# All expert weights split within a layer's first sums, by halves, and shorter layer ends

## What is computed

```python
h = x @ W_in + b_in                                  # 3125 x 256
for l in range(3):
    agg = segment_sum(h[src], dst) / deg
    logits = concatenate([h, agg], -1) @ router_W[l] + router_b[l]
    vals, idx = top_k(logits, 2); gates = softmax(vals)      # over 8 experts
    weak = relu(einsum('nh,ehf->nef', agg, weak_W[l]) + weak_b[l])          # 4 experts, 256 -> 256
    sh = relu(einsum('nh,ehf->nef', agg, strong_W1[l]) + strong_b1[l])      # 4 experts, 256 -> 512
    strong = einsum('nef,efh->neh', sh, strong_W2[l]) + strong_b2[l]        # 512 -> 256
    moe = einsum('ne,neh->nh', gate_dense, concatenate([weak, strong], 1))
    h = h + sigmoid(h @ conf_W[l] + conf_b[l]) * moe
out = h @ W_out + b_out
```

## Time and profile before

| | us |
|---|---|
| median of 3 runs | 3216.36 (3214.8 to 3218.52) |
| the profiled execution | 3218.61, its span 3216.3 |
| granted TensorE clock, mean | 0.975 of full |
| PE busy | 2951.0 (92%) |
| DVE busy | 2189.7 (68%) |
| ACT busy | 914.5 (28%) |

### The profile page before, as it was taken

How to read it: one execution, slowest core, us unless ns; L and a number is a source line. 1 busy time by engine, 2 the same in 40 slices (tenths; PEclk the granted TensorE clock), 3 DMA queues, 4 the chain that set the end, 5 groups by cost and what they waited for, 6 DMA issues and landing times. The chain is left out here.

```text
span 3216.3 us, 47575 instructions
## 1 busy us (share of the span) xinstructions
PE 2951.0 (92%) x18761; PEld 1780.5 (55%) x18761; DVE 2189.7 (68%) x4024; ACT 914.5 (28%) x1695; POOL 18.1 (1%) x23
## 2 busy tenths in 40 slices
PE   2888889999988999999979999988999998999997
PEld 2566555555443545454545666654666664666665
DVE  7999555557227777776657767675767675676676
ACT  3788421114101000000032222233222233232222
POOL 2000000000000000000000000000000000000000
PEclk8899999999998999999989999999999999999999
DMA  5455366775006554544330000020000001000001
GB/s 127 139 151 150 110 192 210 223 230 165 22 9 184 157 171 150 182 145 127 88 106 3 4 3 4 3 82 4 4 7 4 3 27 60 3 4 3 4 3 42
DMA packets 310959, 265.85 MB, mean 83 GB/s; under 512 B 32767, under 2 KB 289409, under 8 KB 308174
## 3 DMA queue, kind: packets, MB, share of 16 engines
q1 hardware_dynamic: 296558, 259.28, 26.3%
q10 hardware_dynamic: 13760, 2.61, 0.4%
q0 software_dynamic: 416, 0.85, 0.1%
HBM read 172.67 MB, written 90.05 MB: 82 GB/s over the span
## 5 line engine op out<-in xcount | busy, mean ns | idle before, releaser
L1874 PE MATMUL psum<-r_wd,r_h 128*128 128x512 fp8e4 (+1 forms) x2600 | 568.4, 375 | 13.4 <-ACT r_h L229 12.9
L2483 PE MATMUL psum<-m_weights,x_nodes 128*128 128x256 f16 (+1 forms) x3600 | 419.7, 275 | 18.0 <-DVE m_wtmp L2267 16.4
L2464 PE MATMUL psum<-m_agg,m_weights 128*128 128x512 f16 (+2 forms) x2016 | 410.3, 356 | 21.7 <-ACT m_agg L2364 21.7
L2422 PE MATMUL psum<-counts,m_h 128*128 128x512 fp8e4 (+2 forms) x2100 | 417.6, 354 | 12.6 <-DVE m_h L2153 12.6
L1874 PEld LDWEIGHTS psum<-r_wd,r_h 128*128 128x128 f16 x2600 | 241.4, 97 | 307.5 <-issue 16.0
L2483 PEld LDWEIGHTS psum<-m_weights,x_nodes 128*128 128x128 f16 (+1 forms) x3600 | 353.7, 99 | 73.3 <-DVE m_wtmp L2267 16.5
L2422 PEld LDWEIGHTS psum<-counts,m_h 128*128 128x128 f16 x2100 | 206.2, 99 | 206.0 <-issue 18.8
L2364 ACT ACTIVATE m_agg<-psum,x_nodes 128x512 f32<-128x512 f32 (+2 forms) x336 | 238.2, 719 | 279.2 <-PE psum L2464 271.2
L2464 PEld LDWEIGHTS psum<-m_agg,m_weights 128*128 128x128 f16 x2016 | 194.9, 99 | 218.8 <-issue 32.7
L2376 ACT ACTIVATE m_hT<-m_hT,m_g 128x256 f32<-128x256 f32 x300 | 135.8, 502 | 552.4 <-DVE m_hT L2281 552.4
L2267 DVE SCALAR_TENSOR_TENSOR m_wtmp<-psum,x_nodes,m_bias 128x256 f32<-128x256 f32 (+1 forms) x300 | 144.9, 483 | 139.0 <-PE psum L2483 137.9
(11 more groups left out here) (312 smaller groups left out, 3328.3 us busy)
## 6 DMA issues: line engine op xcount, KB each, us to landing
r_wd<-packed_sym SPq DMA_DIRECT2D x120, 640.0 KB, 4.1
packed_counts<-strip SPq DMA_DIRECT2D x21, 1800.0 KB, 7.8
sym_blocks<-packed_counts SPq DMA_DIRECT2D x88, 384.0 KB, 4.4
packed_sym<-sym_blocks SPq DMA_DIRECT2D x84, 384.0 KB, 3.3
w_stage<-in_L_gnn_strong_W SPq DMA_DIRECT2D x12, 1024.0 KB, 6.6
m_weights<-in_L_gnn_strong_W SPq DMA_DIRECT2D x21, 512.0 KB, 4.7
x_parked<-x_nodes SPq DMA_DIRECT2D x2, 1600.0 KB, 5.9
x_nodes<-x_parked SPq DMA_DIRECT2D x2, 1600.0 KB, 6.5
```

Of the source, the lines that this page charges most:

```text
L1874: m = pe.matmul(bank[pair[b]][:, 0:2 * cw], h16[:, part, p0 + i, :], f_[:, 2 * b:2 * b + 2, :], start=(p0 + i == 0 and part == 0), stop=(p ...
L2422: m = pe.matmul(bank[kb][:, 0:cw], h16[:, part, i, kb * P:(kb + 1) * P], A[:, i, c_:c_ + cw], start=(i == 0 and part == 0), stop=(i == NT ...
L2464: m = pe.matmul(bank[4 + hh % 2][:, 0:cw], w_[:, i, kb, f * P:(f + 1) * P], agg16[:, j, kb, 0:cw], start=(x_ == 0), stop=(x_ == len(todo) ...
L2483: m = pe.matmul(bank[b_][0:r_, 0:H], s_[:, pa[0] * BANK + k * P:pa[0] * BANK + k * P + r_], w_[:, pa[1], f, :], start=(f == 0 and pa == PA ...
```

## The change

It does five things, all in `block_experts`:

1. All ten pieces of the weights are split within the first sums, on DVE behind the split of h and ahead of the scales and biases, on ACT ahead of the mean. Nothing is split in chunk 0.
2. Each piece is split by halves of 512 columns, two instructions on each engine. ACT's piece k waits only for the low part of the first half of piece k-1.
3. The scale takes one matmul (the maxima, spread to 128 columns, as weights; the identity moving) and one reduction over 128 columns on all partitions. ACT waits for the scale alone, not for the numbers made after it.
4. `turn(0)` moves ahead of the scale on PE and on ACT, and h is split in groups of 2, 3, 5, 5, 5, 5 tiles.
5. In the last chunk DVE's routing is cut in three: hidden blocks 0 and 1, first choice, block 2, second choice, block 3, gates. ACT does its four hidden blocks and then the exponential. And the maximum of the last chunk is taken tile by tile, each behind its last strong tile.

```diff
-                FIRST = 4
+                HALVES = (slice(0, SL // 2), slice(SL // 2, SL))
...
-                H5 = [slice(i, i + 5) for i in range(0, NT, 5)]
+                HG = [slice(i, j) for i, j in zip((0, 2, 5, 10, 15, 20), (2, 5, 10, 15, 20, NT))]
...
-                    vec.wait_ge(max_turned, l + 1)
-                    vec.tensor_reduce(sc[0:1, 1:2], bank[6][0:1, 0:P], axis=AX.X, op=ALU.max).then_inc(steps.handle, steps.up())
-                    mark["h_max_all", l] = steps.n
                     vec.wait_ge(max_spread, l + 1)
-                    vec.tensor_copy(sc[:, 0:1], bank[7][:, 0:1]).then_inc(steps.handle, steps.up())
+                    vec.tensor_reduce(sc[:, 0:1], bank[7][:, 0:P], axis=AX.X, op=ALU.max).then_inc(steps.handle, steps.up())
                     settle()
                     power_scale(sc[:, 0:1], sc[:, 1:2], sc[:, 2:3], sc[:, 3:4])
+
+                    mark["h_scale", l] = steps.n - 1
...
-                        vec.wait_ge(w_high, l * NPC + k + 1)
-                        vec.scalar_tensor_tensor(flat[:, 1, :], loaded_piece(k), scale_of(l, n_, wsc), flat[:, 0, :], ALU.mult,
-                                                 ALU.subtract).then_inc(w_low, 1)
+                        for x_, c_ in enumerate(HALVES):
+                            vec.wait_ge(w_high, 2 * (l * NPC + k) + x_ + 1)
+                            if k and x_ == 0:
+
+                                vec.wait_ge(w_low, 2 * (l * NPC + k))
+                            vec.scalar_tensor_tensor(flat[:, 1, c_], loaded_piece(k)[:, c_], scale_of(l, n_, wsc), flat[:, 0, c_], ALU.mult,
+                                                     ALU.subtract).then_inc(w_low, 1)
...
-                    for k in range(FIRST):
+                    for k in range(NPC):
                         split_low(k)
...
-                        if not more:
+                        if more:
+                            hidden(ci, 0, range(FB))
                             route(ci)
-                        hidden(ci, 0, range(FB))
-                        if more:
-                            route(ci)
-                        if ci == 0:
-                            for k in range(FIRST, NPC):
-                                split_low(k)
+                        else:
+
+                            hidden(ci, 0, range(FB - 2))
+                            route(ci, [0])
+                            hidden(ci, 0, [FB - 2])
+                            route(ci, [1])
+                            hidden(ci, 0, [FB - 1])
+                            route(ci, [2])
...
+                        else:
+                            for i, k in ts:
+                                strong(ci, NSG - 1, [(i, k)])
+                                vec.tensor_reduce(hmax[:, ci + k:ci + k + 1], h2[:, i, :], axis=AX.X, op=ALU.max,
+                                                  apply_absolute_value=True).then_inc(steps.handle, steps.up())
...
                         if k:
-                            act.wait_ge(w_low, l * NPC + k)
-                        act.activation(flat[:, 0, :], loaded_piece(k), ACT.Copy, scale=scale_of(l, ORDER[k][0], wsc)).then_inc(w_high, 1)
+
+                            act.wait_ge(w_low, 2 * (l * NPC + k) - 1)
+                        for c_ in HALVES:
+                            act.activation(flat[:, 0, c_], loaded_piece(k)[:, c_], ACT.Copy, scale=scale_of(l, ORDER[k][0], wsc)).then_inc(w_high, 1)
...
-                    for k in range(FIRST):
+                    for k in range(NPC):
                         split_high(k)
-                    turn(0)
                     mean(0)
...
-                    pe.wait_ge(steps.handle, mark["h_max", l])
-                    pe.transpose(bank[6][0:1, 0:P], sc[:, 0:1], ident[:]).then_inc(max_turned, 1)
-                    pe.wait_ge(steps.handle, mark["h_max_all", l])
-                    pe.matmul(bank[7][:, 0:1], ones_f[0:1, :], sc[0:1, 1:2], start=True, stop=True).then_inc(max_spread, 1)
-                    pe.wait_ge(steps.handle, mark["h_scale", l])
...
+                    turn(0)
+
+                    pe.wait_ge(steps.handle, mark["h_max", l])
+                    pe.matmul(bank[7][:, 0:P], sc[:, 0:1].to_broadcast([P, P]), ident[:], start=True, stop=True).then_inc(max_spread, 1)
                     edges(0)
-                    turn(0)
```

More of the change, by code:

```diff
@@ L2065, in block_experts @@
                 PARTS = ((0, 0), (0, 1), (1, 0))
-                H5 = [slice(i, i + 5) for i in range(0, NT, 5)]
+                HG = [slice(i, j) for i, j in zip((0, 2, 5, 10, 15, 20), (2, 5, 10, 15, 20, NT))]
+                GROUP_AT = {s.start: g for g, s in enumerate(HG)}
                 CUTS_E = [range(0, 5), range(5, 10), range(10, 15), range(15, NT)]
@@ L2338, in turn @@
                             act.activation(hT[:, kb, 0:wd_], bank[2 + kb][:, 0:wd_], ACT.Copy).then_inc(h_kept, 1)
+                    turn(0)
+                    act.wait_ge(steps.handle, mark["h_scale", l])
+                    for s in HG:
+                        act.activation(h16[:, 0, s, :], h2[:, s, :], ACT.Copy, scale=sc[:, 1:2]).then_inc(e_high, 1)
                     def mean(ci):
```

142 lines of the change are left out of this document (71 added, 71 removed).

## The result

| kernel | median, us | range, us | ratio to before, 95% interval | profiled execution | its span |
|---|---|---|---|---|---|
| before (beside it) | 3217.4 | 3214.8 to 3218.9 | | 3218.6 | 3216.3 |
| changed | 3182.3 | 3178.6 to 3183.3 | 0.989 (0.9878 to 0.9902) | 3183.3 | 3181.2 |

The change saves 35.1 us. The forecast was 3180, from 3167 to 3194: time, sign and main mechanism came out as written. That the time is so close is partly luck. The layer ends and starts, together with the last chunks, came out 4.2 us better than forecast (2.7 us won, not 1.5 lost), and the trace has 6.7 us of slow clock that the forecast doesn't have; the two nearly cancel.

The account below looks back on a forecast made before the run. The prediction took PE to bound the expert network nearly everywhere. Its terms, 37.8 - 0.8 - 2.5 + 0.3 + 1.5 = 36.3 us, took the median from 3216.4 to 3180, range 3167 to 3194.

Parts of the forecast that it names:

- First chunk, 37.8 us: Stretch after each layer's first hidden sum: falls to 23.4 us without the waits, saving 37.8 us over three layers.
- Part 1: All ten weight pieces split, by halves, in a layer's first sums; credited with 37.8 us in the first chunks.
- rival (b): First chunk: middle waits only shrink, DVE still late to free the bank, some 5 us a layer missing, 3195; 7%.
- 1.61 us a piece: Splitting in the first sums: halves overlap on DVE and ACT, 1.61 us a piece instead of 2.56, 16.0 for ten.
- Rival (c): Splitting: ACT and DVE halves, both on the same room of weights, slow each other; 3228 at 3.2 us a piece; 3%.
- Rival (a): Splitting: the halves don't overlap, 2.56 us a piece, 28.5 us given back, 3208; 6%.
- Starts, -0.8 us: The three layer starts together: 0.6 us gained in layer 1, 0.3 in layer 2, 1.75 lost in layer 0.
- clock behind the new wait, -2.5: Half clock after PE's new wait: bounds 0 and 1.7 us a layer, half taken, 2.5 us lost over three.
- a new wait of some 2.5 to 3.3 us: PE, after its first sum, waits 2.5 to 3.3 us for the mean to free its bank before the next edge sums.
- Last chunk, 0.5 us a layer: Cut routing in the last chunk: 1.6 to 2.0 us won if the clock holds; 0.5 a layer taken, +1.5 us.
- Part 2: Shorter layer ends, by a shorter way around the scale and a split last maximum; +0.3 us after layer 2.
- part 3: Last chunk's routing in three parts between hidden blocks; some 4.2 us of PE wait moved, +1.5 us in all.

Follow-up runs that it names:

- experiment 2: Kernel before with only the halves and all ten pieces split in the first sums, bias steps behind them; old scale and last chunk: 3182.39 us.
- experiment 1: Changed kernel without the halves: whole pieces of 1024 columns, all ten still split in the first sums: 3212.07 us.
- old_last_route: Same run as experiment 4: changed kernel with the last chunk's routing in one piece ahead of the hidden blocks, as before: 3182.2 us.
- experiment 4: Same run as old_last_route: changed kernel with the last chunk's routing in one piece ahead of the hidden blocks, on DVE and ACT: 3182.2 us.
- experiment 7: Changed kernel with PE doing the last chunk's weak tile between the second and third strong tile: 3179.34 us.
- experiment 8: On top of experiment 7, ACT takes the two hidden blocks ahead of the weak tile's relus in the last chunk: 3174.61 us.
- experiment 3: Changed kernel with the old way around the scale, groups of 5 tiles, turn(0) behind edges(0), one maximum for the last chunk: 3179.16 us.
- best: Changed kernel with bias steps behind the mean, router run broken by edge sums, and PE's weak tile order of experiment 7: 3168.31 us.

## Why the prediction was right, and where it wasn't

**First chunk, 37.8 us: right, 37.9 measured.** Part 1 alone gives the same 219.5 us for the three first chunks (experiment 2). Adding up the same work from later in the chunk gave a stretch of 23.4 us, and it takes 23.37. That DVE would not be late next was right too (16.1 us of work forecast, 16.3 measured); rival (b) is out, for PE is busy in all 23.37 us. One reading was wrong, without harm to the sum: not half of the 12.8 us was idle time but three quarters (36.20 less 26.74 is 9.5), and the half clock made the remaining 3.3.

**1.61 us a piece: right, 1.60 measured;** ten take 15.8 us in layer 0 (1641.86 to 1657.68), 16.0 forecast. A half takes DVE 0.75 us; 0.76 had come from the 618-column rows and the whole piece. So the rows were the better guide than the estimate of 1.34 us made from the page "VectorE: DVE Perf Modes" of the Trainium skill. Rival (c) is out by the same rows. Rival (a) is shown by experiment 1: at 2.56 us a piece the time is 3212, against 3208 worked out.

**Starts, -0.8 us, and clock behind the new wait, -2.5: too pessimistic.** The step that came out wrong is "a new wait of some 2.5 to 3.3 us": it measured 1.78, 0.58 and 0.54. It was shortened from both sides. To compare the two traces in layer 1, I take the start of the last maximum as common point, 2148.28 and 2137.24 in the changed kernel, 11.04 us apart. In the time of the trace before, ACT begins to scale at 2150.4 (forecast 2150.7), DVE's scaling ends at 2159.1 (2159.8), the splits at 2174.9 (2175.8), and the bank is free at 2177.3 (2178.3): each of the four steps adds 0.1 to 0.4 us, all on one side. And PE's first sum ends at 2176.7, not between 2175 and 2176: it starts 2.6 us sooner than before (2141.05 against 2154.70), but takes 24.59 us and not 23.52, since more of it is at half clock. Busy time in the changed kernel there:

```profile
2140.00:2142.00 2.00, 0.95 (x3) 0.43 (x4) 1.77 (x2) 2.00 (x3) 0.00 (x0) 0.51 0.79 259
...
2144.00:2146.00 2.00, 2.00 (x6) 0.72 (x5) 2.00 (x2) 2.00 (x3) 0.00 (x0) 0.50 0.23 90
2146.00:2148.00 2.00, 2.00 (x9) 0.79 (x8) 2.00 (x2) 1.10 (x2) 0.00 (x0) 0.79 0.00 0
```

PE is at the 1.2 GHz level until past 2146, so 1.1 of the 2.6 us go at once. The wait takes up whatever PE wins: in `old_last_route` PE's first sums took 23.26 and 23.09 us, the waits were 1.92 and 2.09, and the stretch from the scale to the first hidden sum was 36.95 and 36.94 us, as in the changed kernel. So that DVE's list ends the first sums is shown, and the wait's length hangs on PE's clock. The half clock that I charged behind the new wait didn't come at all, behind 2.09 us neither. From the scale's start to the next first hidden sum (without the last chunk) layers 1 and 2 gain 1.1 and 0.8 us, and layer 0 loses 0.7 (forecast 1.4 to 2.1), together +1.3 where I had -0.8 - 2.5 = -3.3.

**Last chunk, 0.5 us a layer: the moved wait is right, the gain isn't shown.** From the chunk's start to the next scale (to the output in layer 2) it is 48.05, 47.02 and 47.37 us, against 47.98, 47.63 and 48.34: -0.1, +0.6 and +1.0, together 1.5, where parts 2 and 3 had 1.8. "Some 4.2 us of wait, moved and not removed" measured 3.86, 3.87 and 3.87, with the half clock behind it. But experiment 4 shows that without part 3 the time is the same, and chunks with the same code differ by over 1 us, so that the sum of 1.5 fits is luck. Experiments 7 and 8 show what holds this chunk: PE's order alone moves the wait, and with ACT's order too it shrinks to 1.42 us.

**Part 2, +0.3 us at the end and what the starts hold of it: undersized.** Experiments 2 to 4 give it some 4.8 us of ends and starts, twice. Single executions of one code differ by up to 0.9 us there, so it is more than that scatter, but its size is rough.

**Not foreseen: the spells in chunks 3 and 5, -6.7 us.** The trace before had two of them (7.03 where 5.34 is normal), in stretches that I read only as sums: 393.7 us busy of 396.1 said "PE is the bound", and busy time doesn't show the clock. The mean granted clock of a 396 us stretch rounds such a spell away. A spell is 1.7 us and there are six places, so my range should have held ±5 us for them from the start. It did, by luck, from other terms.

**Sum.** Forecast 36.3; measured 37.9 for the first chunks, 1.3 for the starts, 1.5 for the last chunks and the end, -6.7 for spells, and 1.2 ahead of the experts: 35.2, which is 35.1 but for a remainder of 0.1 in the output's part.

**Open.** Why two equal runs of small matmuls are followed by full clock once and by half clock another time. That breaking or shortening the run removes all spells is shown, and that runs of 16 bring none; what in the run brings them is not. Also open is where in the untouched stages two executions differ by 5.75 us, and why the two waits of 2.64 and 2.63 us in a last chunk (experiment 7, `best`) were followed by half clock once and by full clock once, in each of six chunks.

## What to carry to other kernels

A dependent pair of steps on two engines, with one buffer between pieces, alternates; cut each piece in two and the engines overlap, at the price of the fixed part of each instruction, and rows of two other sizes gave the period of the halves to 0.01 us. Before crediting a moved wait, walk through the lists of all engines in the new order: here a wait went from one line to the next three times. PE's list alone gave nothing, and PE's and ACT's together gave 1.3 to 2.3 us a layer change. And compare the durations of equal groups (24 matmuls in 5.34 or 7.03 us) along the whole trace, since a stretch that is 100% busy can still be at half clock.

## What the hardware showed unexpectedly

- The granted clock fell to its lower level while PE was busy without a gap, behind runs of matmuls with 9 moving columns in f32: 24 matmuls of 512 columns then took 7.03 us, not 5.34. 2 to 6 places of 6 were hit, depending on the execution, and none once groups of 6 edge matmuls stood in the run or it was halved. Runs of 16 such matmuls were never followed by half clock (30 of 30 in the ten traces with the whole run).
- In the expert layers, waits of PE for the mean, a bank or a split of 0.5 to 2.1 us were followed by full clock. Of twelve waits of 2.63 or 2.64 us six were followed by half clock (12 matmuls 3.26 us, not 1.74) and six by full clock. Of 36 waits of 3.79 to 4.88 us within chunks 34 were followed by half clock (12 matmuls 4.17 us, not 2.75). So the same wait can have either behind it.
- ACT and DVE in the same room of weights at once did not slow each other: DVE's half took 0.75 us in the overlapping stream, and the rows of 618 and 1024 columns without that stream give 0.76 for 512.
